# First norm's sums, first loads, context products and VectorE's own operands moved in a two-layer gated transformer kernel

## The chip, the cores and the metric

The kernel runs on one core of a Trainium2 chip, as one program of five instruction streams: TensorE (PE), VectorE (DVE), ScalarE (ACT), GpSimd (POOL) and SyncE (SP), which here only issues transfers. The metric is device time in microseconds, the median of three runs. The profile is of one execution, with a time of its own.

## The reference

x is 128 × 64 tokens of 128 features; four sublayers are added to it, each scaled by tanh of a gate.

```python
x = x + tanh(g_xattn[0]) * L0_xattn(layernorm(x), ctx, ctx)     # 16 heads of 8, among the heads of one token
x = x + tanh(g_ffn[0])   * L0_ffn(layernorm(x))                 # 8 experts, relu, two per token by a hash
x = x + tanh(g_xattn[1]) * L1_xattn(layernorm(x), ctx)          # 64 tokens against 64 of context
x = x + tanh(g_ffn[1])   * L1_ffn(layernorm(x))                 # 8 gated experts + 2 shared, top 2
# L0_xattn, per token l:  q = x Wq, k = ctx Wk, v = ctx Wv, as 16 heads of 8
attn = softmax(einsum('nlhd,nled->nlhe', q, k) / sqrt(8)); out = einsum('nlhe,nled->nlhd', attn, v) @ Wo.T + bo
# L1_xattn:  vk, vv from x;  lk, lv from ctx
a = softmax(vk @ lk.T * 128**-0.5);  out = a @ lv + a @ (a.T @ vv)
```

The first attention compares the 16 heads of one token with one another, so it is no matrix product: each token has 16 × 16 × 8 products for the scores and as many for the values.

## The kernel before

The 8192 tokens are 16 chunks of 512, each four tiles of 128 tokens. The program is unrolled by steps called halves (a tick is two). Every engine walks the same halves, and in each its own short list of calls, so the written order is the order of its instructions; semaphores join the engines.

**Attention.** Half 16(s+1)+k does step k of chunk s. Beside it stands the preparation of chunk p = s+1 (norm, queries, keys and values) and the tail of chunk r = s−1 (output product, residual, second norm, choice of experts). Of the four tiles GpSimd makes three with products of 128x2048: scores by `times_k` (L574), values by `times_v` (L586), through two buffers named prod, so that each product waits until the last but one is reduced. VectorE reduces them (L873 scores, L898 values) and makes the fourth tile itself (`own_times_k` L854, `own_times_v` L862). For that tile keys and values stand in PSUM: `own_keys_values` (L846) copies them there. VectorE also does the statistics of all norms: for the first norm at k = 2, L817 to L827, through PSUM (named YD). GpSimd raises the variance to the power −1/2 (L562) and scatters rows by expert (L596). The four blocks are of chunks up to 3, 7, 11, 15; at each end VectorE computes a table.

**Experts of the first layer** run in twelve steps per block, placed in halves 108 to 356, on TensorE (L1276, L1290) with relus on ScalarE (L683).

**Second layer.** Chunk c's cross attention (C) starts at half 272 + 16c; its context products are lk (L1391) and lv (L1415, beside L1416 in one bank). The gated experts (D) start at half 288 + 16d: up and gate products (L1244 to L1246), silu on ScalarE (L705), hidden product on VectorE (L1095), output (L1328), and for every unit the weighted sum on VectorE (L1110). While C and D of neighbouring chunks overlap, TensorE goes from one to the other by this order alone.

**Start.** SyncE issues eight loads (L453 to L460) and four stores of zeros (L463); TensorE waits for all weights and constants first.

Names: x0 the chunk's rows, q_sb queries and later values' sums, s scores, kv_sb keys and values, MA and MC the banks of the attention's products, xrow the rows of the residual, nmean, ve and rstd a norm's mean (negative), variance and its root's inverse, x3 and xd the D stage's input and sum.

## Time and profile before

| | |
|---|---|
| median of three runs | 1307.96 us (1305.18 to 1308.02) |
| profiled execution | 1305.32 us, its span 1303.6 us |
| granted TensorE clock, mean | 0.959 |
| PE busy | 1113.0 us (85%) |
| DVE busy | 1010.9 us (78%) |
| ACT busy | 586.5 us (45%) |
| POOL busy | 637.0 us (49%) |

The shares are means over stages with different limits, so they are to be read by stretch: attention alone up to about 223 us, attention beside experts to 623 us, then the second layer. "Idle before, releaser" in a row is the time for which the engine had nothing to do, and what ended it.

### The profile page before, as it was taken

Reading aid. Unit: us, or ns where it says so; the run is one execution under the profiler, and the core shown is the slowest. Engines: PE = TensorE matmul, PEld = TensorE weight load, DVE = VectorE, ACT = ScalarE, POOL = GpSimd, SP = SyncE. Lnnn points to the kernel's source line nnn. Section 1 sums busy time; section 2 is a strip of 40 time slices with the busy share of each in tenths; the row PEclk is TensorE's granted clock in tenths of the full one; section 3 lists DMA queues with packets and bytes.
Section 4 is the critical chain, followed back from the end, with each engine's and each line's share of the span. In section 5 each row is a group of like instructions: output and inputs, shape, how many; then the busy total and the mean of one; then the engine's idle time right before and its main releaser. Section 6 shows DMA issues by size and latency. Waiting matters only on the chain.

```text
span 1303.6 us, 23736 instructions
## 1 busy us (share of the span) xinstructions
PE 1113.0 (85%) x7464; PEld 960.2 (74%) x7464; DVE 1010.9 (78%) x2393; ACT 586.5 (45%) x1506; POOL 637.0 (49%) x377
## 2 busy tenths in 40 slices
PE   5145544899969998799889999999999999999998
PEld 3133333789858988688788888889888888888887
DVE  2999999989999899898537444445688888888887
ACT  2212222465636555355454645454344444444443
POOL 4889997898788987899340110101011111111200
PEclk9999985799989999799899999999999999999999
DMA  6101112889748886589666255552000000000000
GB/s 226 49 25 41 40 41 73 264 269 284 224 151 263 278 253 208 187 240 294 189 198 206 78 176 160 174 162 79 22 25 25 25 25 25 26 25 25 26 9 17
DMA packets 125035, 166.41 MB, mean 128 GB/s; under 512 B 10032, under 2 KB 67568, under 8 KB 124912
## 3 DMA queue, kind: packets, MB, share of 16 engines
q1 hardware_dynamic: 119792, 152.31, 38.1%
q0 software_dynamic: 5120, 12.59, 2.9%
q8 instruction: 61, 1.00, 0.3%
q14 instruction: 62, 0.51, 0.1%
HBM read 137.60 MB, written 27.26 MB: 126 GB/s over the span
## 4 chain that ended last, share of the span: by engine, by line
PE 56%; DVE 25%; issue 8%; POOL 7%; ACT 2%; DMA 1%; SPq 0%; DVEq 0%; POOLq 0%; ACTq 0%
PE ZB L1276 8%; DVE q_sb L898 6%; PE YB L1290 6%; PE YD L1328 5%; DVE s L873 4%; PE ZD L1244 4%; PE ZD L1246 4%; PE ZD L1245 4%; POOL prod L586 3%; PE YB L1328 3%; PE ZB L1244 2%; DVE own_prod L862 2%; PE ZB L1246 2%; PE ZB L1245 2%; POOL xs L596 2%
## 5 line engine op out<-in xcount | busy, mean ns | idle before, releaser
L562 POOL TENSOR_TENSOR rstd<-ve,neghalf 128x4 f32<-128x4 f32 x64 | 65.6, 1025 | 516.6 <-DVE ve L827 515.2
L683 ACT ACTIVATE hid<-ZB,w2b 128x128 f32<-128x128 f32 x768 | 215.8, 378 | 159.0 <-PE YB L1290 78.5
L574 POOL TENSOR_TENSOR prod<-q_sb,kv_sb 128x2048 f32<-128x2048 f32 x48 | 216.3, 4507 | 51.9 <-DVE q_sb L898 31.6
L586 POOL TENSOR_TENSOR prod<-s,kv_sb 128x2048 f32<-128x2048 f32 x48 | 215.2, 4505 | 10.6 <-DVE q_sb L898 10.5
L1276 PE MATMUL ZB<-bt,w1b 128*128 128x128 f32 x1536 | 213.2, 284 | 4.9 <-ACT hid L683 4.7
L1276 PEld LDWEIGHTS ZB<-bt,w1b 128*128 128x128 f32 x1536 | 197.0, 200 | 8.5 <-issue 8.0
L1290 PE MATMUL YB<-w2b,hid 128*128 128x128 f32 x1024 | 141.4, 282 | 0.0
L1290 PEld LDWEIGHTS YB<-w2b,hid 128*128 128x128 f32 x1024 | 129.1, 194 | 14.2 <-ACT hid L683 8.0
L705 ACT ACTIVATE own_prod<-ZD 128x512 f32<-128x512 f32 x102 | 61.1, 599 | 154.6 <-PE ZD L1246 152.3
L1095 DVE TENSOR_TENSOR prod<-own_prod,ZD 128x512 f32<-128x512 f32 x102 | 69.5, 682 | 75.0 <-ACT own_prod L705 51.7
L1110 DVE SCALAR_TENSOR_TENSOR own_prod<-YD,gate,own_prod 128x128 f32<-128x128 f32 x320 | 89.7, 342 | 46.5 <-PE YD L1328 44.6
L873 DVE TENSOR_REDUCE s<-prod 128x256 f32<-128x2048 f32 x48 | 108.2, 2275 | 5.4 <-POOL prod L574 5.4
L898 DVE TENSOR_REDUCE q_sb<-prod 128x128 f32<-128x2048 f32 x48 | 109.1, 2273 | 1.4 <-POOL prod L586 1.0
L1244 PE MATMUL ZD<-ut_hi,w_hi 128*128 128x512 f32 x204 | 89.0, 436 | 0.0
L1328 PEld LDWEIGHTS YD<-w2u_sb,prod 128*128 128x128 f32 x640 | 79.8, 192 | 9.9 <-issue 4.7
L1328 PE MATMUL YD<-w2u_sb,prod 128*128 128x128 f32 x640 | 85.0, 276 | 2.4 <-DVE own_prod L1110 1.5
L1246 PE MATMUL ZD<-ut_lo,w_hi 128*128 128x512 f32 x204 | 80.5, 394 | 0.0
L1245 PE MATMUL ZD<-ut_hi,w_lo 128*128 128x512 f32 x204 | 80.4, 394 | 0.0
L596 POOL DMA_INDIRECT xs<-xrow,slots x64 | 63.3, 989 | 23.1 <-issue 17.7
L608 POOL DMA_INDIRECT x<-x2d,homes x64 | 61.8, 966 | 23.6 <-issue 23.3
L1290 PE MATMUL ZD<-w2b,hid 128*128 128x128 f32 x512 | 69.3, 279 | 0.0
L1290 PEld LDWEIGHTS ZD<-w2b,hid 128*128 128x128 f32 x512 | 62.6, 192 | 5.8 <-issue 3.0
(249 smaller groups left out, 2321.0 us busy)
## 6 DMA issues: line engine op xcount, KB each, us to landing
w2b<-in_w SPq DMA_DIRECT2D x96, 516.0 KB
w1b<-in_w SPq DMA_DIRECT2D x96, 512.0 KB
xb<-xs SPq DMA_DIRECT2D x96, 128.0 KB
ctx_t<-in_ctx SPq DMA_DIRECT2D x32, 256.0 KB
x2d<-x2s SPq DMA_DIRECT2D x48, 128.0 KB
x<-in_x SPq DMA_DIRECT2D x16, 256.0 KB
xs<-zrow SPq DMA_DIRECT2D x4, 1024.0 KB, 10.5
xrow<-in_x SPq DMA_DIRECT2D x16, 256.0 KB, 3.6
```

The lines of the kernel that those rows point to most:

```text
L574: pool.tensor_tensor(out=prod[:, t % 2, :].rearrange("p (h e d) -> p h e d", h=HEADS, e=HEADS), in0=q.unsqueeze(2).broadcast_to([P, HEADS, ...
L586: pool.tensor_tensor(out=prod[:, (t + 1) % 2, :].rearrange("p (h d e) -> p h d e", h=HEADS, e=HEADS), in0=s0[:, t, :, :].unsqueeze(2).broa ...
L683: act.activation(hid[n % 2][:, j, k * RT:(k + 1) * RT], ZB[j // 2][:, at:at + RT], ACT.Relu, bias=w2b[t % 3][:, k, e, FJ * D + j:FJ * D + ...
L873: dve.tensor_reduce(out=s0[:, t, :, :].rearrange("p h e -> p (h e)"), in_=src.rearrange("p (g d) -> p g d", d=HD), axis=X, op=ALU.add).the ...
L898: dve.tensor_reduce(out=o_sb[a % 2][:, t, :], in_=src.rearrange("p (g e) -> p g e", e=HEADS), axis=X, op=ALU.add).then_inc(av_sum.sem, 1)
L1110: last = dve.scalar_tensor_tensor(out=xd[:, j, :], in0=b[:, j * P:(j + 1) * P], scalar=gate[:, j, u - SHARED:u - SHARED + 1], in1=xd[:, j, ...
L1244: pe.matmul(dst, l_hi, r_hi, start=True, stop=False)
L1245: pe.matmul(dst, l_lo, r_hi, start=False, stop=False)
L1246: return pe.matmul(dst, l_hi, r_lo, start=False, stop=True)
L1276: last = pe.matmul(ZB[j // 2][:, at:at + RT], w1b[t % 2][:, k, e, j * P:(j + 1) * P], bt[t % 2][:, k * RT:(k + 1) * RT], start=True, stop= ...
L1290: last = pe.matmul(b[:, k * D:(k + 1) * D], hid[n % 2][:, f, k * RT:(k + 1) * RT], w2b[t % 3][:, k, e, f * D:(f + 1) * D], start=False, st ...
L1328: last = pe.matmul(b[:, js], hu[(d * UNITS + u) % 3][:, js], w2u_sb[:, u, :], start=True, stop=True)
```

## The change

1. The order of the first loads: rows, biases, context and 384 columns of the weights first, the rest behind them. The zero stores go to halves 24 to 36, the constants of VectorE to half 16, and TensorE's wait for the other weights to half 24. The first chunk has an order of its own.
2. For chunks from 1 on ScalarE makes the first norm's sums: `sums_of_rows` at k = 12 of the step before, `sums_of_squares` at k = 0. VectorE turns them into mean and variance with two operations of 128x4.
3. VectorE's own keys and values are read from kv_sb, which ScalarE now fills for all four tiles; `own_keys_values` goes. The choice of experts needs two operations less.
4. The context products of all 16 chunks are made in halves 31 to 91 (`languages`), stored to DRAM (lk_d, lv_d) and loaded in C.
5. In D from chunk 5 on, ScalarE weighs units 2 to 5 (`unit_weighed`), GpSimd adds them (`add_unit`), and VectorE's other sums come one half later.

```diff
+LANG_AT = [16 * (c // 4) + 31 + (0, 2, 9, 12)[c % 4] for c in range(NC)]
+LANG = {half: c for c, half in enumerate(LANG_AT)}
...
+BY_ACT = (2, 3, 4, 5)
+WEIGHED = {(d, u): (d - FIRST_ACT) * len(BY_ACT) + i + 1 for d in range(FIRST_ACT, NC) for i, u in enumerate(BY_ACT)}
+STEP = {}
+for _d in range(NC):
+    for _u in range(1, UNITS):
+        if (_d, _u) not in WEIGHED:
+            STEP[_d, _u] = len(STEP) + 1
...
+            sp.dma_start(x0[:], x_v[0]).then_inc(ld_x.sem, 16)
+            sp.dma_start(bias_raw[:], bias_rows[0:BG].unsqueeze(0)).then_inc(s_bias, 16)
+            sp.dma_start(ctx_t[:], ctx_in[:, 0:CH]).then_inc(ld_ca.sem, 16)
+            sp.dma_start(ws[:, 0:WO], w_small[:, 0:WO]).then_inc(s_ws, 16)
...
-            sp.dma_start(x0[:], x_v[0]).then_inc(ld_x.sem, 16)
-            sp.dma_start(ctx_t[:], ctx_in[:, 0:CH]).then_inc(ld_ca.sem, 16)
-            sp.dma_start(ws[:], w_small).then_inc(s_ws, 16)
+            sp.wait_ge(s_ws, 16)
+            sp.dma_start(ws[:, WO:WSMALL], w_small[:, WO:WSMALL]).then_inc(s_ws, 16)
...
-            for b in range(len(BLOCKS)):
-                sp.dma_start(xs[b][8 * GT * RT:ROWS].rearrange("(k p) d -> p k d", p=P),
-                             zrow[:].unsqueeze(1).broadcast_to([P, SPARE, 2 * D])).then_inc(st_zero.sem, 16)
...
                 if k == 9 and has(p + 1):
                     filled(sp, "xt0", p)
                     sp.dma_start(x0[:], x_v[p + 1]).then_inc(ld_x.sem, 16)
+                if 24 <= half < 24 + 4 * len(BLOCKS) and half % 4 == 0:
+                    sp.dma_start(xs[half // 4 - 6][8 * GT * RT:ROWS].rearrange("(k p) d -> p k d", p=P),
+                                 zrow[:].unsqueeze(1).broadcast_to([P, SPARE, 2 * D])).then_inc(st_zero.sem, 16)
...
+                for c in range(NC):
+                    if half == (LANG_AT[c - 2] + 1 if has(c - 2) else LANG_AT[c] - 4):
+                        if has(c - 2):
+                            sp.wait_ge(pe_lang.sem, pe_lang.at(c - 2))
+                        sp.dma_start(ctx_l[c % 2], ctx_in[:, c * CH:(c + 1) * CH]).then_inc(ld_cl[c % 2].sem, 16)
...
+                    sp.dma_start(lk_d[c], lang_k[c % 2]).then_inc(st_lang[c % 2].sem, 16)
+                    sp.dma_start(lv_d[c], lang_v[c % 2]).then_inc(st_lang[c % 2].sem, 16)
...
-                                filled(sp, "val", c - 1)
-                            sp.dma_start(ctx2_t[:], ctx_in[:, c * CH:(c + 1) * CH]).then_inc(ld_cc.sem, 16)
+                                filled(sp, "sc", c - 1)
...
+                            sp.dma_start(lk_t[:], lk_d[c]).then_inc(ld_lk.sem, 16)
+                            if has(c - 1):
+                                emptied(sp, "val", c - 1)
+                            sp.dma_start(lv_sb[:], lv_d[c]).then_inc(ld_lv.sem, 16)
...
+            def add_unit(d, u):
+                n = WEIGHED[d, u]
+                if u == BY_ACT[0]:
+                    pool.wait_ge(xd_s.sem, STEP[d, 1])
+                else:
+                    pool.wait_ge(added.sem, n - 1)
+                pool.wait_ge(y_s.sem, n)
+                pool.tensor_tensor(out=xd[:], in0=xd[:], in1=y_act[n % 2][:], op=ALU.add).then_inc(added.sem, 1)
...
+            def sums_of_rows(c):
+                if has(c - 1):
+                    act.wait_ge(ln_stats[0].sem, ln_stats[0].at(c - 1))
+                act.wait_ge(ld_x.sem, ld_x.at(c))
+                for j in range(TILES):
+                    last = act.activation(spill[:, j, :], x0[:, j, :], ACT.Copy, accum_out=sums0[:, 0, j:j + 1])
+                last.then_inc(sums0_s.sem, 1)
+            def sums_of_squares(c):
+                act.wait_ge(ln_stats[0].sem, ln_stats[0].at(c, 1))
+                for j in range(TILES):
+                    last = act.activation(spill[:, j, :], x0[:, j, :], ACT.Square, bias=nmean[:, 0, j:j + 1], accum_out=sums0[:, 1, j:j + 1])
+                last.then_inc(sums0_s.sem, 1)
...
+                if half and has(p - 2):
+                    act.wait_ge(own_av.sem, own_av.at(p - 2))
+                act.activation(kv_sb[p % 2][:, 2 * half:2 * half + 2, :].rearrange("p j d -> p (j d)"), b[:],
+                               ACT.Copy).then_inc(free_of(f"kv{half}", p), 1)
...
+                act.wait_ge(pe_f.sem, pe_f.at(d, u))
+                b = unit_sums[SUM[d, u][0]]
+                for j in range(TILES):
+                    last = act.activation(y_act[n % 2][:, j, :], b[:, j * P:(j + 1) * P], ACT.Copy, scale=gate[:, j, u - SHARED:u - SHARED + 1])
+                last.then_inc(y_s.sem, 1)
...
                     plain(ot[:], "ot", r)
+                if half == 4:
+                    normed(0, lambda j: xn0[:, j, :], lambda j: x0[:, j, :], 0)
...
+                if half == 14:
+                    weights()
...
+                if k == 12 and has(p + 1):
+                    sums_of_rows(p + 1)
+                if k == 0 and has(p) and p > 0:
+                    sums_of_squares(p)
...
+            def later_consts():
...
+            def means_of_rows(c):
+                dve.wait_ge(sums0_s.sem, sums0_s.at(c - 1, 1))
+                dve.wait_ge(ln_rstd[0].sem, ln_rstd[0].at(c - 1))
+                dve.tensor_scalar(nmean[:, 0, :], sums0[:, 0, :], -1.0 / D, None, ALU.mult).then_inc(ln_stats[0].sem, 1)
+            def variances_of_rows(c):
+                dve.wait_ge(sums0_s.sem, sums0_s.at(c - 1))
+                dve.tensor_scalar(ve[:, 0, :], sums0[:, 1, :], 1.0 / D, EPS, ALU.mult, ALU.add).then_inc(ln_stats[0].sem, 2)
...
-            def own_keys_values(p):
-                kv_part_of = filled(dve, "kv1", p)
-                dve.wait_ge(kv_part.sem, kv_part.at(p))
-                if has(p - 1):
-                    dve.wait_ge(own_av.sem, own_av.at(p - 1))
-                dve.tensor_copy(kv_own, kv_part_of[:, (PT - 2) * 2 * D:2 * 2 * D]).then_inc(free_of("kv1", p), 1)
...
-                kk = kv_own[:, 0:D].rearrange("p (e d) -> p e d", e=HEADS)
+                kk = kv_sb[a % 2][:, PT, 0:D].rearrange("p (e d) -> p e d", e=HEADS)
...
-                v = kv_own[:, D:2 * D].rearrange("p (d e) -> p d e", e=HEADS)
+                v = kv_sb[a % 2][:, PT, D:2 * D].rearrange("p (d e) -> p d e", e=HEADS)
...
-                hs = sm("hsum").unsqueeze(2).broadcast_to([P, TILES, TRUNC_MAX])
-                th_ = thr[:].unsqueeze(1).broadcast_to([P, TILES, TRUNC_MAX])
-                dve.tensor_tensor(out=hge[:], in0=hs, in1=th_, op=ALU.is_ge).then_inc(s, 1)
-                dve.scalar_tensor_tensor(out=hle, in0=hs, scalar=-1.0, in1=th_, op0=ALU.mult, op1=ALU.is_ge).then_inc(s, 1)
+                hs = sm("hsum").unsqueeze(2).broadcast_to([P, TILES, 2 * TRUNC_MAX])
+                th_ = thr[:].unsqueeze(1).broadcast_to([P, TILES, 2 * TRUNC_MAX])
+                dve.tensor_tensor(out=hge[:], in0=hs, in1=th_, op=ALU.is_gt).then_inc(s, 1)
+                dve.wait_ge(pick.sem, pick.at(r, 2))
+                dve.tensor_reduce(out=sm("htr"), in_=hge[:], axis=X, op=ALU.add).then_inc(s, 1)
...
+                dve.wait_ge(ld_lv.sem, ld_lv.at(c))
+                dve.tensor_tensor(out=u_sb[:], in0=tiles(b), in1=tiles(lv_sb), op=ALU.add).then_inc(free_of("val", c), 1)
...
+                back = 1 if d >= FIRST_ACT else 0
+                if UNIT_OUT.get(pos) == 1:
+                    unit_sum(d, 1)
+                elif (d, UNIT_OUT.get(pos - back)) in STEP and UNIT_OUT[pos - back] > 1:
+                    unit_sum(d, UNIT_OUT[pos - back])
...
+                if half == 16:
+                    later_consts()
...
-                    if has(p):
-                        dve.wait_ge(ld_x.sem, ld_x.at(p))
-                        norm_stats(0, lambda j: x0[:, j, :], p)
+                    if has(p) and p > 0:
+                        variances_of_rows(p)
...
+                if k == 14 and has(p + 1):
+                    means_of_rows(p + 1)
...
-                    if has(p):
-                        own_keys_values(p)
...
-                    pe.wait_ge(xd_s.sem, earlier + 1)
+                    if earlier in WEIGHED:
+                        pe.wait_ge(y_s.sem, WEIGHED[earlier])
+                    else:
+                        pe.wait_ge(xd_s.sem, STEP[earlier])
...
+            def languages(c):
...
+                pe.wait_ge(ld_cl[c % 2].sem, ld_cl[c % 2].at(c // 2))
+                pe.matmul(ZB[0][:], ws[:, WLK:WLK + P], ctx_l[c % 2], start=True, stop=True).then_inc(pe_lang.sem, 1)
+                bias_rows_of(ZB[1][:, :], BLV, D, TILES)
+                by_token(ZB[1], ctx_l[c % 2], WLV, D, start=False).then_inc(pe_lang.sem, 1)
...
-                        pe.matmul(b[:, js], ctx2_t[:, js], ws[:, WLV:WLV + D], start=True, stop=False)
-                        last = pe.matmul(b[:, js], blockdiag[:, j, :], vv_sb[:, j, :], start=False, stop=True)
+                        last = pe.matmul(b[:, js], blockdiag[:, j, :], vv_sb[:, j, :], start=True, stop=True)
...
-            pe.wait_ge(s_rows, 16)
-            pe.wait_ge(s_dve0, DVE_CONSTS)
-            pe.wait_ge(s_w2u, 16)
+            pe.wait_ge(s_dve0, 1)
...
+                if half == 24:
+                    pe.wait_ge(s_ws, 32)
+                    pe.wait_ge(s_dve0, DVE_CONSTS)
+                    pe.wait_ge(s_w2u, 16)
+                if half in LANG:
+                    languages(LANG[half])
```

VectorE in an attention cycle, behind its own value product, to the reciprocal and the copy. Before:

```order
L862 TENSOR_TENSOR own_prod<-s,YD 128x2048 [waits exp0]
L906 TENSOR_TENSOR q_sb<-q_sb,YD 128x256 [waits rec0_s,av_sum]
L888 TENSOR_REDUCE sum<-s 128x32 [waits exp0]
L890 RECIPROCAL YD<-sum 128x32 [waits rec0_s]
L846 COPY YD<-MC 128x256 [waits own_av,kv_part,mc_full]
```

and now:

```order
L978 TENSOR_TENSOR own_prod<-s,kv_sb 128x2048 [waits exp0]
L946 TENSOR_SCALAR nmean<-sums 128x4 [waits ln_rstd0,sums0_ready]
L1022 TENSOR_TENSOR q_sb<-q_sb,YD 128x256 [waits rec0_s,av_sum]
L1004 TENSOR_REDUCE sum<-s 128x32 [waits exp0]
L1006 RECIPROCAL YD<-sum 128x32 [waits rec0_s]
```

The mean of the next chunk stands directly behind the value product, and the copy is gone.

VectorE a few instructions on, from the reduction of its own value product to the first reductions of scores (YD is in PSUM, stats and sums in SBUF). Before:

```order
L898 TENSOR_REDUCE q_sb<-own_prod 128x128 [waits own_av]
L906 TENSOR_TENSOR q_sb<-q_sb,YD 128x256 [waits rec0_s,av_sum]
L817 BN_STATS stats<-x 128x6 [waits ld_x]
L817 BN_STATS stats<-x 128x6 x3
L821 BN_AGGR YD<-stats 128x2 [waits ln_stats0]
L821 BN_AGGR YD<-stats 128x2 x3
L826 TENSOR_SCALAR nmean<-YD 128x4 [waits ln_rstd0,ln_stats0]
L827 TENSOR_SCALAR ve<-YD 128x4
L873 TENSOR_REDUCE s<-prod 128x256 [waits pool_qk] x2
```

and now:

```order
L1014 TENSOR_REDUCE q_sb<-prod 128x128 [waits pool_av]
L1014 TENSOR_REDUCE q_sb<-own_prod 128x128 [waits own_av]
L1022 TENSOR_TENSOR q_sb<-q_sb,YD 128x256 [waits rec0_s,av_sum]
L950 TENSOR_SCALAR ve<-sums 128x4 [waits sums0_ready]
L989 TENSOR_REDUCE s<-prod 128x256 [waits pool_qk] x2
```

Seven instructions' worth of statistics became one operation, with both sides in SBUF.

TensorE in the last stage, where the next chunk's cross attention begins (prod and xn are norm outputs, transposed here; L1391 is lk). Before:

```order
L1235 MATMUL MC<-ident,prod 128x128 [waits ln_done3,mc_free]
L1235 MATMUL MC<-ident,prod 128x128 x3
L1391 MATMUL MA<-ctx_t,ws 128x512 [waits ld_ctx_c,ma_free]
L1328 MATMUL YB<-w2u_sb,prod 128x128 [waits hu_ready,xd_step]
L1328 MATMUL YB<-w2u_sb,prod 128x128 x3
L1235 MATMUL MC<-ident,xn 128x128 [waits ln_done2,mc_free]
L1235 MATMUL MC<-ident,xn 128x128 x3
```

and now:

```order
L1362 MATMUL MA<-ident,prod 128x128 [waits ln_done3,ma_free]
L1362 MATMUL MA<-ident,prod 128x128 x3
L1460 MATMUL YB<-w2u_sb,prod 128x128 [waits hu_ready,xd_step]
L1460 MATMUL YB<-w2u_sb,prod 128x128 x3
L1362 MATMUL MC<-ident,xn 128x128 [waits ln_done2,mc_free]
L1362 MATMUL MC<-ident,xn 128x128 x3
L1460 MATMUL YD<-w2u_sb,prod 128x128 [waits hu_ready,xd_step]
```

The product lk is gone between the two transposes; some of the L1460 products now wait for y_by_act instead of xd_step.

## Rows read from the trace of the kernel before

**Rows 1.** Busy time by stretch: stretch, us; PE, PEld, DVE, ACT, POOL, PEclk, DMA, GB/s

```profile
38.00:183.00 145.00, 66.98 (x200) 45.92 (x200) 139.61 (x209) 31.73 (x66) 129.08 (x54) 1.00 0.13 39
...
700.00:913.00 213.00, 209.12 (x1554) 187.62 (x1554) 104.77 (x330) 106.42 (x297) 25.26 (x32) 1.00 0.49 150
948.00:1272.00 324.00, 314.87 (x2126) 271.89 (x2125) 263.88 (x866) 153.36 (x271) 58.20 (x75) 1.00 0.09 24
```

**Rows 2.** Timeline of POOL: start us, us, engine, line, operation, idle before

```profile
38.31 4.51 POOL L586 TENSOR_TENSOR prod<-s,kv_sb 128x2048 f32<-128x2048 f32 x1
...
147.94 13.36 POOL L586 TENSOR_TENSOR prod<-s,kv_sb 128x2048 f32<-128x2048 f32 x3
161.26 9.04 POOL L574 TENSOR_TENSOR prod<-q_sb,kv_sb 128x2048 f32<-128x2048 f32 x2
...
172.12 4.51 POOL L574 TENSOR_TENSOR prod<-q_sb,kv_sb 128x2048 f32<-128x2048 f32 x1 [0.57 <-DVE s L873]
...
182.96 4.49 POOL L586 TENSOR_TENSOR prod<-s,kv_sb 128x2048 f32<-128x2048 f32 x1
...
223.21 13.36 POOL L586 TENSOR_TENSOR prod<-s,kv_sb 128x2048 f32<-128x2048 f32 x3
...
377.63 13.41 POOL L586 TENSOR_TENSOR prod<-s,kv_sb 128x2048 f32<-128x2048 f32 x3
...
532.18 8.96 POOL L586 TENSOR_TENSOR prod<-s,kv_sb 128x2048 f32<-128x2048 f32 x2
...
570.82 4.52 POOL L586 TENSOR_TENSOR prod<-s,kv_sb 128x2048 f32<-128x2048 f32 x1
```

**Rows 3.** Timeline of DVE over the same cycle

```profile
159.09 2.28 DVE L862 TENSOR_TENSOR own_prod<-s,YD 128x2048 f32<-128x2048 f32 x1
161.29 0.41 DVE L906 TENSOR_TENSOR q_sb<-q_sb,YD 128x256 f32<-128x256 f32 x1
...
162.60 0.37 DVE L846 COPY YD<-MC 128x256 f32<-128x256 f32 x1
162.88 0.18 DVE L950 TENSOR_TENSOR spick<-MA,oh_all 128x32 f32<-128x32 f32 x1
...
163.40 2.27 DVE L898 TENSOR_REDUCE q_sb<-prod 128x128 f32<-128x2048 f32 x1
...
168.24 0.86 DVE L817 BATCH_NORM_STATS2 stats<-x 128x6 f32<-128x128 f32 x4
...
169.70 4.47 DVE L873 TENSOR_REDUCE s<-prod 128x256 f32<-128x2048 f32 x2
```

**Rows 4.** Line L922: its durations (min/median/max), and one of them on DVE's timeline

```profile
L922 DVE COPY oh_all<-base x4: 155/257/2229, 84.4 to 542.3; 128x8 f32<-128x8 f32 x4
...
229.93 2.23 DVE L922 COPY oh_all<-base 128x8 f32<-128x8 f32 x1
```

**Rows 5.** Timelines of SP, PE and POOL at the start

```profile
4.85 9.30 SPq L463 DMA_DIRECT2D xs<-zrow  x4
...
11.03 0.76 PE L1341 MATMUL MC<-bias_hi,ones_r 1*128 1x512 f32 x1 [11.03 <-DMA w2u_sb<-in_w2u]
...
23.73 4.49 POOL L574 TENSOR_TENSOR prod<-q_sb,kv_sb 128x2048 f32<-128x2048 f32 x1 [10.14 <-ACT q_sb L661]
```

**Rows 6.** Timelines of PE and ACT in the last stage

```profile
1000.86 0.38 PE L1415 MATMUL MC<-ws,ctx_t 128*128 128x128 f32 x2
1001.07 0.39 PE L1416 MATMUL MC<-vv_sb,blockdiag 128*128 128x128 f32 x2
...
1013.12 1.02 PE L1391 MATMUL MA<-ctx_t,ws 128*128 128x512 f32 x2
...
1015.59 0.63 PE L1235 MATMUL MC<-ident,xn 128*128 128x128 f32 x4 [0.56 <-ACT xn L655]
...
1013.81 1.63 ACT L655 ACTIVATE xn<-x,nmr,rstd 128x128 f32<-128x128 f32 x4
```

**Rows 7.** Timeline of SP beside the experts

```profile
342.76 0.44 SPq L475 DMA_DIRECT2D x<-in_x  x1
```

More of the change, by code:

```diff
@@ L469, in _ @@
                 p, a, r = s + 1, s, s - 1
[L470 removed]
+                if k == (7 if p > 0 else 10) and has(p + 1):
                     filled(sp, "kv1", p)
@@ L637, in _ @@
                             gather(c, (2, 3))
+                for d, kd in d_parts(tick):
+                    u = UNIT_OUT.get(2 * kd + later - 1)
+                    if (d, u) in WEIGHED:
+                        add_unit(d, u)
         @block.scalar
```

158 lines of the change are left out of this document (99 added, 59 removed).

## The prediction

> **What bounds the kernel now.** I read the table of stretches first [rows 1], then the timelines of GpSimd (POOL) and VectorE (DVE) over one attention cycle [rows 2, 3], one odd instruction of VectorE [rows 4], the start [rows 5], and TensorE (PE) in the last stage [rows 6]. The table splits the program in two. In 38 to 183 us VectorE is busy 139.6 of 145 us and GpSimd 129.1, TensorE only 67: attention is a two-engine loop. From 700 us on TensorE decides alone: 209.1 of 213 us, and 314.9 of 324 in the last stage [rows 1].
>
> The loop's period is the distance between two first value products of GpSimd, 147.94 to 182.96: 35.02 us, and nothing but this loop runs there. Each product takes 4.45 us. Three of values run back to back from 147.94, two of keys follow at 161.26, the third of keys starts only at 172.12, after 0.57 us of waiting for VectorE's reduction L873 [rows 2]. VectorE in turn waits only some tenths per cycle for a product. So both engines are within 0.6 us of being the bound, and whatever delays either one in this loop is paid in full.
>
> **The change, part by part.**
>
> 1. *VectorE's work per chunk shrinks.* Gone are the norm statistics of the first norm (168.24 to 169.70, 1.46 us), the copy L846 (162.60 to 162.88, 0.28 us) [rows 3] and two of the small operations of the expert choice, about 0.27 us in all. Two operations of 128x4 are added, means_of_rows behind own_times_v and variances_of_rows behind head_scale. By start-to-start time they cost 0.08 us each, an estimate from their size. Taken alone this is 1.85 us less on VectorE, of which GpSimd's own loop (35.02 less its 0.57 wait) lets through about 0.6 us a chunk.
>
> 2. *But the two new operations have another form.* The old ones read PSUM; the new ones read SBUF and write SBUF. The trace has one operation of that kind inside attention, the copy L922, four times, each 128x8: 155 ns at the least, 257 in the middle, 2229 at the most [rows 4]. The long one started at 229.93 on VectorE. GpSimd had started three value products at 223.21, each 4.45 us, so its second ended at 223.21 + 8.9 = 232.1, and the copy ended at 229.93 + 2.23 = 232.16. It read as a wait until GpSimd's product was over. I take it that a one-source operation from SBUF to SBUF waits for the running product, and apply this to both new operations.
>
> Where do they fall? Before, own_times_v started at 159.09 and the next operation at 161.29; GpSimd's first key product started at 161.26 [rows 2, 3]. The new means_of_rows takes the place at 161.29, 0.03 us too late: it waits for the key product, to 161.26 + 4.5 = 165.7, which is 4.4 us. The tail behind it (161.29 to 163.40, less the copy 0.28: 1.83 us) then ends at 167.5, and the third reduction of values at 167.5 + 2.2 = 169.7. GpSimd's second key product waits for that reduction since it reuses its buffer: it starts at 169.8, not at 165.7. Reduction of the own product and scale bring VectorE to 172.3; there variances_of_rows finds that second product running, until 174.2. The first reduction of key products ends at 174.3 + 2.2 = 176.5, and with it the third key product starts at about 176.6, not at 172.12. That is 4.5 us late, and the cycle grows from 35.02 to about 39.6, **+4.6 us**.
>
> The waits act where a chunk two ahead exists, so in 14 of 15 intervals between first value products. By groups:
> - The first three intervals, 38.31 to 147.94 [rows 2]: 109.6 us, 4.6 over three bare cycles of 35.02. Half of that excess I take as covered by the new waits: 3 × 4.6 − 2.3 = +11.5.
> - One bare interval (147.94 to 182.96): +4.6. One with the block's table (182.96 to 223.21, 40.25 us): +4.4.
> - Two blocks of four intervals beside the experts, 223.21 to 377.63 and on to 532.18: 154.4 us each, 14.3 over four bare cycles. The table's 5.2 of it stays; of the other 9.1, which are waits for other engines, 2.4 stays as an estimate: 4 × 39.6 + 7.6 = 166.0, so +11.6 each, +23.2.
> - The last one (532.18 to 570.82, 38.6 us) to 40.3: +1.7.
>
> Sum for attention: 11.5 + 4.6 + 4.4 + 23.2 + 1.7 = **+45.4 us**.
>
> 3. *VectorE's own products now take both operands from SBUF.* No row shows such an operation beside a product of GpSimd; before, one operand was always in PSUM. Bounds: nothing, as the same operation runs at 2.2 us now, or a wait like that of L922, which is rival A below. I take nothing, since the rows show the wait only for a one-source form.
>
> The Trainium skill ("SBUF — State Buffer", section "Who interferes with whom") says more: a VectorE instruction with two SBUF inputs, or a one-source one that can use both ports, shares an exclusive port pair with GpSimd, and whoever comes second is blocked entirely. The second half agrees with the 2229 ns of L922; the first half speaks against this change and no row here shows it. With it the result would be rival A's.
>
> 4. *ScalarE (ACT) makes the sums.* Eight passes of 128x128 per chunk, 1.63 us for four [rows 6]: 3.3 us on an engine that is under half busy, hidden in the free stretches. Beside the experts it can hurt: the load of x is issued at 342.76 in the place where ScalarE makes relus without a break [rows 7], and sums_of_rows stands ahead of relus in its queue. An x that lands some 3 to 4 us later holds them, and with them TensorE. Bounds 0 to 8 us over all chunks. In the main case VectorE is late by more than that, so I take 0; in rival C it counts 8.
>
> 5. *Start.* TensorE starts at 11.03, after the last of the eight first loads; the first key product at 23.73; SyncE's queue is held 9.3 us by four stores of zeros [rows 5]. With 384 columns of the weights awaited instead of everything, TensorE can start about 5 us earlier, and the queries are made before the second half of keys and values, which takes 2 us more out of the chain: **−7 us** (5 to 9). The weights deferred are needed at half 24, behind the first products. The four stores of zeros move to halves 24 to 36; the first that waits for them is SyncE's padding at the end of the first block, so nothing is late by it. On SyncE's queue they now stand among loads of context and x that are issued early, which I cost at nothing, with 1 us as the bound.
>
> 6. *Context products.* lk (two passes, 1013.12 to 1013.98, 0.86 us) and lv (four passes of 0.22, as 1000.86 to 1001.07 [rows 6], 0.9 us) leave each of 16 late chunks and go where TensorE is half idle; 28 us are hidden there, with ScalarE's copies. In the five chunks before the last stage, where TensorE is 98% busy, they save 5 × 1.76 = 8.8; I take 7.5, since some of these chunks overlap waits. In the last stage lk saves nothing: behind it TensorE waits 0.56 us for ScalarE's xn at 1015.59 [rows 6], and would wait 1.4 instead. lv saves 0.9 less what the new hand-over costs.
>
> 7. *Units weighed by ScalarE and added by GpSimd.* This takes four operations from VectorE for each of four units. VectorE is not the bound there (263.9 of 324 us [rows 1]). TensorE now waits for ScalarE's 1.63 us instead of VectorE's similar step, with one half less of room, and I charge 0.3 us a chunk: 11 × (0.9 − 0.3) = −6.6. Bounds −12 to +5. Parts 6 and 7 together: **−14 us**.
>
> Sum against the profiled run's own 1305.3 us: 45.4 − 7 − 14.1 = +24.3, so 1329.6. The median of the runs lies 2.7 over the profiled one, so the forecast is **1332 us**.
>
> **Rivals.**
>
> *A, both forms wait.* own_times_v at 159.09 waits for the third value product until 161.26 and keeps GpSimd out to 163.5; GpSimd's key product runs 163.5 to 168.0, and means_of_rows behind it to 168.0. That is 2.3 us more than in the main case; own_times_k, beside GpSimd's power of the variance before the next value product, adds 0.7: cycle 42.6, +3.0 on the main case. 3 × 3.0 + 2 × 3.0 + 8 × 3.0 + 3.0 = 42 on top: **1374 us**. For it: copy L846 pays 0.28 us a chunk [rows 3] for nothing but an operand in PSUM. Against: no row shows such a wait.
>
> *B, the tie is won.* means_of_rows gets in ahead of the key product at 161.26; the two starts lie 0.03 us apart. Then it waits for nothing, variances_of_rows waits 2.3 us, most of it behind GpSimd's own loop; the cycle is 35.4: about +5 in attention, **1292 us**. From a lead of 0.03 us it decides for each cycle.
>
> *C, no waits* (the other side: faster). The 2.23 us of L922 had another cause. Attention gives 14 × 0.6 = 8 us, which ScalarE's late x takes back (part 4); start −7, parts 6 and 7 −14: 1305.3 − 21 + 2.7 = **1287 us**. For it: VectorE's saved 1.85 us a chunk is real. Against: the end of L922 fits GpSimd's to 0.1 us.
>
> **How the numbers follow.** Main case 0.30 (own range 1318 to 1348: each wait may be 1 us shorter, the D stage may give nothing), A 0.28, B 0.12, C 0.30. Predicted is the main case, 1332. The range takes in A and C: C less 6 for ScalarE's stalls not coming, 1281; A plus 14 for the last stage giving nothing, 1388. A change of 0.3%, 4 us, is about what can be told from none. Slower is main and A, 0.57 with a 0.01 from them near zero; faster is B and C less 0.04 where their savings fail, 0.38; within 0.3% 0.05.
>
> **What would show it.** The two operations of 128x4 at means_of_rows and variances_of_rows: near 0.15 us each in B's and C's case, medians of 4.4 and 1.9 us in mine. own_times_v: 2.2 us, or 4.4 in A. Distance between first value products in the bare stretch: 39.6, 42.6 (A), 35.4 (B), 34.4 (C). First key product at about 17 us. Last stage: about 0.6 us less a chunk. The forecast is wrong if the first of these is short.

## The result

The changed kernel takes 1404.96 us, median of four runs (1401.13 to 1409.36), against 1306.92 us before (1305.18 to 1308.02): a ratio of 1.0753, with a 95% interval of 1.0717 to 1.0788. It is 98 us slower. The sign was forecast; the size was not: 1332 us was predicted, and 1405 lies above the range's end of 1388.

The profiled execution took 1404.14 us with a span of 1401.8 us. The first view is the source view of lines of the changed kernel: durations in ns, least, median and most, then the first and last start. L946 is the new mean, L950 the new variance, L978 VectorE's own product of values, L970 that of keys, L621 GpSimd's key products, L633 its value products.

```profile
L946 DVE TENSOR_SCALAR nmean<-sums x15: 1668/4437/4466, 16.5 to 651.4; 128x4 f32<-128x4 f32 x15
L950 DVE TENSOR_SCALAR ve<-sums x15: 170/2084/2109, 23.2 to 662.4; 128x4 f32<-128x4 f32 x15
L978 DVE TENSOR_TENSOR own_prod<-s,kv_sb x16: 2281/2850/4384, 47.8 to 737.8; 128x2048 f32<-128x2048 f32 x16
L970 DVE TENSOR_TENSOR own_prod<-q_sb,kv_sb x16: 2279/2282/5914, 34.3 to 713.5; 128x2048 f32<-128x2048 f32 x16
L621 POOL TENSOR_TENSOR prod<-q_sb,kv_sb x48: 4471/4516/6569, 13.6 to 703.7; 128x2048 f32<-128x2048 f32 x48
L633 POOL TENSOR_TENSOR prod<-s,kv_sb x48: 4471/4507/6604, 30.4 to 729.8; 128x2048 f32<-128x2048 f32 x48
```

An operation on 512 numbers takes 4.4 us, and that is the wait which the forecast named. But the two products of VectorE are stretched too, up to 4.4 and 5.9 us, and GpSimd's up to 6.6, which the forecast had put at nothing. The bare cycle (147.94 to 182.96 in the kernel before, beside no experts and no table) shows both. Here are VectorE's and then GpSimd's timeline of the changed kernel in the stretch that answers to [rows 2, 3]:

```profile
174.19 2.29 DVE L1014 TENSOR_REDUCE q_sb<-prod 128x128 f32<-128x2048 f32 x1 [0.43 <-POOL prod L633]
176.39 4.35 DVE L978 TENSOR_TENSOR own_prod<-s,kv_sb 128x2048 f32<-128x2048 f32 x1
180.67 4.45 DVE L946 TENSOR_SCALAR nmean<-sums 128x4 f32<-128x4 f32 x1
185.03 0.41 DVE L1022 TENSOR_TENSOR q_sb<-q_sb,YD 128x256 f32<-128x256 f32 x1
...
191.70 2.08 DVE L950 TENSOR_SCALAR ve<-sums 128x4 f32<-128x4 f32 x1
193.69 4.47 DVE L989 TENSOR_REDUCE s<-prod 128x256 f32<-128x2048 f32 x2
...
203.97 2.28 DVE L970 TENSOR_TENSOR own_prod<-q_sb,kv_sb 128x2048 f32<-128x2048 f32 x1
```

```profile
165.20 13.39 POOL L633 TENSOR_TENSOR prod<-s,kv_sb 128x2048 f32<-128x2048 f32 x3
178.56 6.52 POOL L621 TENSOR_TENSOR prod<-q_sb,kv_sb 128x2048 f32<-128x2048 f32 x1
189.28 4.47 POOL L621 TENSOR_TENSOR prod<-q_sb,kv_sb 128x2048 f32<-128x2048 f32 x1 [4.19 <-DVE q_sb L1014]
...
196.13 4.51 POOL L621 TENSOR_TENSOR prod<-q_sb,kv_sb 128x2048 f32<-128x2048 f32 x1 [0.99 <-DVE s L989]
...
203.46 0.96 POOL L643 DMA_INDIRECT xs<-xrow,slots  x1 [0.30 <-issue]
204.73 2.36 POOL L643 DMA_INDIRECT xs<-xrow,slots  x1 [0.30 <-issue]
207.12 1.04 POOL L608 TENSOR_TENSOR rstd<-ve,neghalf 128x4 f32<-128x4 f32 x1
208.24 0.20 POOL L610 TENSOR_TENSOR nmr<-nmean,rstd 128x4 f32<-128x4 f32 x1
208.39 8.94 POOL L633 TENSOR_TENSOR prod<-s,kv_sb 128x2048 f32<-128x2048 f32 x2
```

Read them side by side. VectorE's product is ready at 176.39, but GpSimd's third value product runs until 178.6: VectorE comes to its next operation at 180.67, 4.3 us later instead of 2.2. GpSimd's key product, ready at 178.56, takes 6.52 us: 2.1 us of waiting for VectorE and 4.4 of work. The mean, ready at 180.67, then waits until this key product is over (185.08), the variance waits from 191.70 to the end of the next (193.75). Three times in a cycle VectorE waits for GpSimd, and twice GpSimd for VectorE: at the key product, and at the last scatter, which takes 2.36 us instead of 0.96 while VectorE makes its product of keys (203.97). The cycle, from 165.20 to 208.39, is 43.2 us; it was 35.02 [rows 2].

By the distances between first value products (L633 here, L586 in rows 2) the whole program divides as follows, in us:

| part | before | changed | difference | forecast |
|---|---|---|---|---|
| up to the first value product | 38.3 | 30.4 | −7.9 | −7 |
| first three intervals | 109.6 | 134.8 | +25.2 | +11.5 |
| bare interval | 35.0 | 43.2 | +8.2 | +4.6 |
| interval with table | 40.2 | 48.4 | +8.1 | +4.4 |
| two blocks of four beside experts | 154.4, 154.6 | 186.3, 192.9 | +70.2 | +23.2 |
| last two intervals | 38.6, 34.2 | 42.9, 37.0 | +7.1 | +1.7 |
| from the last first value product to the end | 698.6 | 686.0 | −12.6 | −14 |

The two parts outside attention came as forecast. All of the miss is in attention, +118.7 us instead of +45.4.

The blocks also show something that the bare cycle doesn't. These rows are of the waits of ScalarE and TensorE in the changed kernel, 250 to 720 us (total, times, longest). L729 is the sum of squares, L756 the relus, L1405 the experts' first product.

```profile
ACT x L729 <- DVE nmean L946: 61.8, 7, 14.5
```

```profile
PE ZB L1405 <- ACT hid L756: 39.7, 17, 5.8
```

ScalarE stood 61.8 us at the sum of squares, waiting for the mean that VectorE brought late, with relus queued behind it; TensorE stood 39.7 us for relus (3.1 us in the kernel before, 223 to 623 us).

And TensorE itself was slower there. These are the two blocks of the kernel before and then of the changed kernel, with the columns of [rows 1]:

```profile
223.21:377.63 154.42, 140.15 (x1013) 124.61 (x1011) 143.40 (x246) 82.65 (x264) 133.19 (x57) 0.93 0.76 234
377.63:532.18 154.55, 141.17 (x1011) 125.11 (x1012) 142.00 (x247) 82.19 (x264) 133.31 (x57) 0.93 0.76 235
```

```profile
256.76:443.03 186.27, 151.47 (x1018) 133.56 (x1018) 170.52 (x203) 94.31 (x328) 148.55 (x57) 0.86 0.62 195
443.03:635.92 192.89, 157.34 (x1015) 138.76 (x1016) 172.63 (x203) 94.63 (x328) 148.97 (x58) 0.82 0.60 189
```

In the kernel before TensorE is busy nine tenths of a block. For nearly the same number of matmuls it is busy 11 and 16 us longer in the changed kernel, at a granted clock of 0.86 and 0.82 instead of 0.93.

### The profile page after: what moved, and what is told of

It is laid out like the page before. It is cut to its first block, busy times and chain, and to the rows that moved or that the text cites. A ratio compares the mean times of both kernels' runs of the same rounds, so it can differ in the third digit from the quotient of the medians.

```text
span 1401.8 us, 24127 instructions
## 1 busy us (share of the span) xinstructions
PE 1180.8 (84%) x7496; PEld 997.6 (71%) x7496; DVE 1083.4 (77%) x2050; ACT 686.3 (49%) x1938; POOL 751.8 (54%) x422
## 3 DMA queue, kind: packets, MB, share of 16 engines
q1 hardware_dynamic: 129154, 169.10, 38.3%
## 4 chain that ended last, share of the span: by engine, by line
PE 52%; DVE 28%; POOL 7%; issue 6%; ACT 3%; SPq 1%; DMA 1%; DVEq 0%; POOLq 0%; another core or an unknown queue 0%; ACTq 0%
PE ZB L1405 8%; PE YB L1419 6%; DVE q_sb L1014 5%; PE YD L1460 5%; DVE nmean L946 4%; DVE s L989 4%; POOL prod L633 4%; DVE own_prod L978 3%; PE ZD L1371 3%; PE ZD L1372 3%; PE ZD L1373 3%; PE YB L1460 3%; DVE own_prod L970 3%; POOL xs L643 2%; PE ZB L1371 2%
## 5 line engine op out<-in xcount | busy, mean ns | idle before, releaser
L621 POOL TENSOR_TENSOR prod<-q_sb,kv_sb 128x2048 f32<-128x2048 f32 x48 | 246.5, 5137 | 96.1 <-DVE q_sb L1014 74.5
L756 ACT ACTIVATE hid<-ZB,w2b 128x128 f32<-128x128 f32 x768 | 216.3, 377 | 139.4 <-PE YB L1419 59.1
L1405 PE MATMUL ZB<-bt,w1b 128*128 128x128 f32 x1536 | 226.2, 296 | 43.4 <-ACT hid L756 43.3
L1405 PEld LDWEIGHTS ZB<-bt,w1b 128*128 128x128 f32 x1536 | 208.5, 211 | 47.7 <-issue 47.3
L633 POOL TENSOR_TENSOR prod<-s,kv_sb 128x2048 f32<-128x2048 f32 x48 | 227.5, 4760 | 17.9 <-DVE q_sb L1014 17.7
L608 POOL TENSOR_TENSOR rstd<-ve,neghalf 128x4 f32<-128x4 f32 x64 | 68.6, 1071 | 267.0 <-DVE ve L941 263.9
L665 POOL TENSOR_TENSOR own_prod<-own_prod,prod 128x512 f32<-128x512 f32 x44 | 56.5, 1285 | 208.6 <-ACT prod L788 208.4
L1014 DVE TENSOR_REDUCE q_sb<-prod 128x128 f32<-128x2048 f32 x48 | 109.0, 2271 | 11.7 <-POOL prod L633 11.6
L1233 DVE SCALAR_TENSOR_TENSOR own_prod<-YD,gate,own_prod 128x128 f32<-128x128 f32 x232 | 65.1, 342 | 40.3 <-PE YD L1460 39.5
L1460 PE MATMUL YD<-w2u_sb,prod 128*128 128x128 f32 x640 | 86.0, 277 | 4.7 <-DVE own_prod L1233 3.8
L1460 PEld LDWEIGHTS YD<-w2u_sb,prod 128*128 128x128 f32 x640 | 79.2, 191 | 9.7 <-DVE own_prod L1233 5.6
L643 POOL DMA_INDIRECT xs<-xrow,slots x64 | 70.7, 1104 | 23.1 <-issue 17.6
L1419 PE MATMUL ZD<-w2b,hid 128*128 128x128 f32 x512 | 76.6, 298 | 0.0
L1419 PEld LDWEIGHTS ZD<-w2b,hid 128*128 128x128 f32 x512 | 69.8, 210 | 6.7 <-issue 3.7
```

The lines of the kernel that those rows point to most:

```text
L621: pool.tensor_tensor(out=prod[:, t % 2, :].rearrange("p (h e d) -> p h e d", h=HEADS, e=HEADS), in0=q.unsqueeze(2).broadcast_to([P, HEADS, ...
L633: pool.tensor_tensor(out=prod[:, (t + 1) % 2, :].rearrange("p (h d e) -> p h d e", h=HEADS, e=HEADS), in0=s0[:, t, :, :].unsqueeze(2).broa ...
L643: pool.indirect_dma_start(xs[b], bass.IndirectOffsetOnAxis(ap=slots[:, r, j:j + 1], axis=0), xrow[r % 2][:, j, :], None).then_inc(st_xs[r ...
L756: act.activation(hid[n % 2][:, j, k * RT:(k + 1) * RT], ZB[j // 2][:, at:at + RT], ACT.Relu, bias=w2b[t % 3][:, k, e, FJ * D + j:FJ * D + ...
L1014: dve.tensor_reduce(out=o_sb[a % 2][:, t, :], in_=src.rearrange("p (g e) -> p g e", e=HEADS), axis=X, op=ALU.add).then_inc(av_sum.sem, 1)
L1405: last = pe.matmul(ZB[j // 2][:, at:at + RT], w1b[t % 2][:, k, e, j * P:(j + 1) * P], bt[t % 2][:, k * RT:(k + 1) * RT], start=True, stop= ...
```

## The experiments

Each kernel was run beside the kernel before. Their statements were written before they ran. The edits are shown against the changed kernel, except where it is said otherwise.

**e1: the own operands in PSUM again, the small operations as changed**

```diff
-                act.activation(kv_sb[p % 2][:, 2 * half:2 * half + 2, :].rearrange("p j d -> p (j d)"), b[:],
-                               ACT.Copy).then_inc(free_of(f"kv{half}", p), 1)
+                n = PT - 2 if half else 2
+                act.activation(kv_sb[p % 2][:, 2 * half:2 * half + n, :].rearrange("p j d -> p (j d)"), b[:, 0:n * 2 * D],
+                               ACT.Copy).then_inc(kv_part.sem if half else free_of(f"kv{half}", p), 1)
...
+                dve.tensor_copy(kv_own, kv_part_of[:, (PT - 2) * 2 * D:2 * 2 * D]).then_inc(free_of("kv1", p), 1)
...
-                kk = kv_sb[a % 2][:, PT, 0:D].rearrange("p (e d) -> p e d", e=HEADS)
+                kk = kv_own[:, 0:D].rearrange("p (e d) -> p e d", e=HEADS)
```

> The changed kernel with VectorE's own keys and values copied to PSUM again (ScalarE copies three tiles, VectorE the fourth), all else as changed. Its products then have one operand in SBUF; the mean and the variance keep both sides in SBUF. Theory 1 (every VectorE operation that reads twice from SBUF, or goes from SBUF to SBUF, shuts out and is shut out by GpSimd's products): only the two small waits are left, own_times_v takes 2.28 us each time, GpSimd's key products 4.5 us at most; bare cycle 39.5 us (43.2 changed, 35.0 before), time about 1405 - 14 x 3.7 = 1353 us. Rival (the small operations alone make all of it, the products' longer times are a mere consequence): the cycle stays at 43, time near 1400.

Measured: 1336.93 us, ratio 1.0243 (1.0226 to 1.026), 16 us less than stated. This is the case that I had forecast for the changed kernel. On VectorE's and GpSimd's timelines:

```profile
165.87 2.28 DVE L985 TENSOR_TENSOR own_prod<-s,YD 128x2048 f32<-128x2048 f32 x1
168.06 4.49 DVE L946 TENSOR_SCALAR nmean<-sums 128x4 f32<-128x4 f32 x1
...
179.41 2.09 DVE L950 TENSOR_SCALAR ve<-sums 128x4 f32<-128x4 f32 x1
```

```profile
154.66 13.42 POOL L634 TENSOR_TENSOR prod<-s,kv_sb 128x2048 f32<-128x2048 f32 x3
168.05 4.47 POOL L622 TENSOR_TENSOR prod<-q_sb,kv_sb 128x2048 f32<-128x2048 f32 x1
176.99 4.48 POOL L622 TENSOR_TENSOR prod<-q_sb,kv_sb 128x2048 f32<-128x2048 f32 x1 [4.47 <-DVE q_sb L1021]
```

The own product takes 2.28 us again and the key product 4.47. The mean is ready at 168.06, GpSimd's key product at 168.05: the tie is lost by 0.01 us, as forecast, and costs 4.4 us. The bare cycle is 40.0 us (forecast 39.6). Over the whole of attention the median wait is shorter, since in the other cycles the mean came up to 1.8 us after the start of the key product; it never came ahead of it:

```profile
L946 DVE TENSOR_SCALAR nmean<-sums x15: 443/3155/4501, 19.3 to 589.7; 128x4 f32<-128x4 f32 x15
```

The rival, that the small operations make all of the loss, falls: 68 us went away with the own operands, where the statement had 52.

**e2: mean and variance with an operand in PSUM, the own operands as changed**

```diff
-                dve.tensor_scalar(nmean[:, 0, :], sums0[:, 0, :], -1.0 / D, None, ALU.mult).then_inc(ln_stats[0].sem, 1)
+                dve.scalar_tensor_tensor(out=nmean[:, 0, :], in0=sums0[:, 0, :], scalar=-1.0 / D, in1=sm("zero"), op0=ALU.mult, op1=ALU.add).then_inc(ln_stats[0].sem, 1)
```

and the variance in the same way with `sm("eps")`; both constants stand in PSUM.

> The changed kernel with mean and variance made by a two-input form whose second input, zero or epsilon, stands in PSUM; VectorE's own products still read SBUF twice. Theory 1: the mean takes 0.2 us instead of 4.4, own_times_v still 2.3 to 4.4 us, GpSimd's first key product up to 6.6; bare cycle 38.1, time about 1405 - 14 x 5.1 = 1334 us. Rival (two-input reads from SBUF cost nothing by themselves): cycle 34.4, own_times_v 2.28 throughout, time about 1283.

Measured: 1328.96 us, ratio 1.0199 (1.0158 to 1.0239); 1334 had been stated. The mean takes 146 ns in the median and at most 158, in the same place of the same queue:

```profile
L950 DVE SCALAR_TENSOR_TENSOR nmean<-sums,YD x15: 143/146/158, 17.4 to 577.7; 128x4 f32<-128x4 f32 x15
L982 DVE TENSOR_TENSOR own_prod<-s,kv_sb x16: 2282/4158/4373, 47.8 to 658.9; 128x2048 f32<-128x2048 f32 x16
```

The own product of values still waits, median 4.2 us. The bare cycle is 37.8 us. So each form waits by itself. The edit changes the kind of operation together with the place of an operand; the kernel before tells them apart. There the first two norms' means were the same TENSOR_SCALAR of 128x4 with its source in PSUM, about half of them begun while a product of GpSimd was running (one at 169.56, beside the product of 161.26 to 170.30), and none took more than 163 ns:

```profile
L826 DVE TENSOR_SCALAR nmean<-YD x32: 160/161/163, 11.9 to 649.7; 128x4 f32<-128x4 f32 x32
```

**e3: both together**

> Both of these together: no operation of VectorE in attention takes two operands from SBUF or goes from SBUF to SBUF, except the table's copy. All other parts of the change stay. Theory 1: bare cycle 34.4, and with the waits of VectorE gone ScalarE's squares don't hold relus for long; time about 1285 us, below the kernel before (1307). Rival (ScalarE's sums in its queue, ahead of relus, cost by themselves in the blocks of experts): bare cycle 34.4, but the blocks stay 5 to 15 us longer than the 154.4 of before, time 1300 to 1315.

Measured: 1291.18 us, ratio 0.9899 (0.9863 to 0.9934), faster than the kernel before. The products and the two small operations are no longer stretched, GpSimd's value products take at most 4.54 us; only the table's copy (L922 before), left as it was, still takes up to 1.80 us.

```profile
L989 DVE TENSOR_TENSOR own_prod<-s,YD x16: 2275/2278/2280, 48.9 to 625.5; 128x2048 f32<-128x2048 f32 x16
```

The two intervals ahead of the table are 35.0 and 36.0 us, not 34.4, and the blocks are 155.4 and 160.0 us. The time is 6 us above the 1285 stated and below the rival's 1300: the waits are gone, and something in the blocks is left.

The four kernels, changed, e1, e2 and e3, differ in two edits alone, so they price what comes of both waits together: 1404.96 − 1336.93 − 1328.96 + 1291.18 = 30 us beyond the sum of each alone. By the distances between first value products 29 of it lie in the two blocks of four.

**e4: as e1, with the first norm's statistics on VectorE again**

```diff
                 if k == 14 and has(p + 1):
-                    means_of_rows(p + 1)
...
-                        variances_of_rows(p)
+                        dve.wait_ge(ld_x.sem, ld_x.at(p))
+                        norm_stats(0, lambda j: x0[:, j, :], p)
```

> As the first kernel of this call (own operands in PSUM), with the first norm's statistics on VectorE again and no sums on ScalarE. What is left of the change: the start, the shorter expert choice, the context products, the units weighed by ScalarE. Theory 1: bare cycle 34.7 to 35.0 as before, blocks as before (154), start and second layer as in the changed kernel, 8 + 12 us less than before: 1287 us. If ScalarE's sums cost in the blocks, this kernel is faster than the third by what they cost; if they only help, it is 0 to 8 us slower.

ScalarE's sums are gone as well. Measured: 1289.72 us, ratio 0.9881 (0.9865 to 0.9898); 1287 had been stated. The same two intervals are 35.8 and 35.1, the blocks 154.3 and 153.9. Without the sums on ScalarE the kernel is as fast as with them: the 1.46 us that they take from VectorE per chunk bring nothing. Where they went is seen in VectorE's largest wait, 38 to 600 us, of the kernel before, of e3 and of e4. It is the residual (xrow) waiting for the attention's output product on TensorE:

```profile
DVE xrow L913 <- PE MA L1240: 10.8, 8, 3.7
```

```profile
DVE xrow L1040 <- PE MA L1380: 40.5, 13, 5.8
```

```profile
DVE xrow L1032 <- PE MA L1371: 17.8, 8, 3.7
```

In e3 VectorE comes to this place earlier and waits 40.5 us in all instead of 10.8 (18.1 with 7.3 us at the same operation for which the view names no engine). I read this as the next limit: the chain of output transpose, copy and product didn't get shorter. No run shortened it, so that is not shown.

**e5: e4 without the units weighed by ScalarE**

```diff
-FIRST_ACT = next(d for d in range(NC) if 2 * C0[d] + 16 > EXPERTS_END + 4)
+FIRST_ACT = NC
```

> As e4_stats_dve, but ScalarE weighs no unit in the last stage; VectorE makes all unit sums again. If the weighing gives nothing (VectorE is not the bound there, my step 7), this is 1286 to 1290 us, as e4 or up to 3 us faster, since TensorE doesn't wait for ScalarE's slower hand-over. Rival (it is what brings the last stage's gain): 1295 or more.

Measured: 1292.53 us, ratio 0.9888 (0.9871 to 0.9904). From the last first value product to the end it takes 690.6 us, e4 685.1, in one execution of each. The medians lie only 2.8 us apart and the intervals of the two ratios overlap, so a gain of 3 to 6 us from the weighing is possible and not shown. What is shown is that it doesn't cost the 3 us with which I had charged it. The time lies between the statement's 1290 and its rival's 1295.

**e6: e4 with lk and lv made in the cross attention, as before**

```diff
-LANG = {half: c for c, half in enumerate(LANG_AT)}
+LANG = {}
...
-C_FIRST = {1: "vk", 2: "vv", 4: "bdt"}
+C_FIRST = {0: "lk", 1: "vk", 2: "vv", 4: "bdt"}
```

> As e4_stats_dve, but the context products lk and lv stay in the cross attention as in the kernel before. If they bring 14 us in the second layer (step 6), the second layer grows by 8 to 14 us and the time is about 1300. In the first chunks the granted clock tells whether these products have to do with its fall to 0.79 (24 to 150 us; 1.00 before): at 1.00 here, they have; attention would then be 1 to 3 us shorter.

Measured: 1302.26 us, ratio 0.9955 (0.9939 to 0.9972). The same last stretch takes 701.5 us, so moving the context products brings 16 us of it beside the weighing (8 to 14 had been stated). The clock answers clearly. These are the rows of the table of stretches, 24 to 150 us, of the kernel before, of e4 and of e6; the number after POOL's is the granted clock:

```profile
24.00:150.00 126.00, 58.01 (x165) 38.79 (x164) 115.25 (x169) 31.14 (x64) 111.92 (x44) 1.00 0.13 38
```

```profile
24.00:150.00 126.00, 94.11 (x304) 57.26 (x304) 119.53 (x178) 44.97 (x87) 108.06 (x44) 0.79 0.46 151
```

```profile
24.00:150.00 126.00, 55.84 (x160) 37.61 (x160) 120.28 (x178) 30.30 (x63) 108.23 (x43) 1.00 0.23 73
```

With the context products there the granted clock of this stretch, a mean between its two levels, is 0.79; without them it is 1.00. But attention from the first to the last first value product takes 566.3 us in e6 and 565.6 in e4, so the lower clock costs nothing that can be seen, where the statement had 1 to 3 us; TensorE is not the limit there.

**e7: the kernel before with the own operands read from SBUF, and nothing else** (the edit is e1's, the other way round)

> The kernel before with this one part of the change: VectorE's own keys and values read from SBUF, ScalarE copying all four tiles, the copy to PSUM gone. Theory 1 (two-input reads from SBUF and GpSimd's products shut each other out): VectorE's product of values 4.35 us instead of 2.28, GpSimd's first key product 6.5, bare cycle 37.8 to 38.5 instead of 35.0, time 1306 + 14 x 3 = 1345 us. Rival (it needs the other parts, as the freed queue slots): no change, 1303.

Measured: 1346.7 us, ratio 1.0314 (1.0265 to 1.0363), as stated. The operand of two products, moved from PSUM to SBUF, costs 39 us, and that although it saves the copy of 0.28 us a chunk. The bare cycle is 38.7 us, just over the 38.5 stated. On GpSimd's timeline there is a second victim; VectorE's own product of keys started at 154.91 (first fence), just ahead of a scatter:

```profile
154.91 2.28 DVE L856 TENSOR_TENSOR own_prod<-q_sb,kv_sb 128x2048 f32<-128x2048 f32 x1
```

```profile
153.97 0.96 POOL L597 DMA_INDIRECT xs<-xrow,slots  x1 [0.30 <-issue]
155.24 2.79 POOL L597 DMA_INDIRECT xs<-xrow,slots  x1 [0.30 <-issue]
158.05 1.05 POOL L562 TENSOR_TENSOR rstd<-ve,neghalf 128x4 f32<-128x4 f32 x1
```

The scatter takes 2.79 us instead of 0.96. In the kernel before, with the operand in PSUM, the same pair ran side by side and the scatter took 0.96:

```profile
180.41 2.28 DVE L854 TENSOR_TENSOR own_prod<-q_sb,YD 128x2048 f32<-128x2048 f32 x1
```

```profile
180.70 0.96 POOL L596 DMA_INDIRECT xs<-xrow,slots  x1 [0.30 <-issue]
```

**e8: e3 with ScalarE's sums for chunks 1 to 6 only**

> As e3_both_psum, but ScalarE makes the first norm's sums only for chunks 1 to 6; from 7 on, where experts run beside attention, VectorE's statistics return. If the sums in ScalarE's queue ahead of relus are what made e3's two expert blocks 155.4 and 160.0 us against 154.3 and 153.9 of e4, these go to 154 to 155 and the time is 1284 to 1288, the fastest of all; if they stay over 157, it was something else.

Measured: 1288.78 us, ratio 0.9856 (0.984 to 0.9872); blocks 155.4 and 156.5 us, both over the 154 to 155 stated. The second block went from 160.0 to 156.5, against 153.9 in e4; the first stayed. So the sums account for 3.5 of the second block's 6.1 us at most, and for nothing in the first; the rest is not explained. It is the lowest ratio of all, but its interval overlaps e4's.

**e9: the changed kernel with the sums of squares one half later**

```diff
-                if k == 0 and has(p) and p > 0:
+                if k == 1 and has(p) and p > 0:
                     sums_of_squares(p)
```

> The changed kernel with ScalarE's sums of squares one half later (k = 1 instead of 0), behind the relus of one more expert step; nothing else moved. In the changed kernel ScalarE waited 61.8 us for the mean there, and TensorE 39.7 us for relus, in 250 to 720 us. If that wait at the head of ScalarE's queue is what the blocks of experts lose beyond the waits between VectorE and GpSimd (186.3 and 192.9 us against 166.7 and 168.0 with the small waits alone), both blocks get 5 to 15 us shorter each, and the time is 1375 to 1395; the bare cycle stays 43.2. If ScalarE's wait is hidden, all stays at 1405.

Measured: 1392.33 us, ratio 1.0669 (1.0648 to 1.069), 12.6 us less than the changed kernel. Blocks 180.2 and 184.8 us, 6 and 8 less. Over 250 to 720 us ScalarE's wait for the mean fell from 61.8 to 15.9 us, TensorE's for relus from 39.7 to 31.6. So ScalarE's wait at the head of its queue does cost, 12.6 us net of what the move itself costs. TensorE's busy time in the blocks fell too, by 5.2 and 4.3 us, at a granted clock of 0.91 and 0.85 instead of 0.86 and 0.82; whether that is a part of the gain or comes of it, no run tells.

**e10: e3 with the same move**

> As e3_both_psum with the same move of the squares. ScalarE waited 24.7 us for the mean there and TensorE 9.0 us for relus. If this is the rest that ScalarE's sums cost, its two blocks go from 155.4 and 160.0 to 154 to 157 and the time to 1286 to 1289 (1291 for e3); if not, no change within 2 us.

Measured: 1300.76 us, ratio 0.9963 (0.9942 to 0.9985): a miss, nearly 10 us slower than e3. Its blocks are 161.8 and 160.7 us. Where VectorE is not late the move has nothing to mend, and it brings the variance, and with it the norm, later. TensorE's wait for relus didn't fall (12.0 us over 200 to 660 us, 9.0 in e3). Which part of the norm's chain makes the 10 us I haven't followed.

## Why the prediction was wrong

**The bound (right).** Attention was read as a loop of two engines within 0.6 us of each other, where every delay is paid in full. Each bare cycle shows it.

**Part 2, the small operations (right; in the bare cycle to 0.5 us).** Forecast 4.4 us for the mean, 1.9 for the variance, cycle 39.6 us. In e1, where they act alone, they take 4.49 and 2.09 in the bare cycle, which is 40.0; the mean's median over all chunks is 3.16. From the first to the last first value product e1 takes 617.2 us, 50.5 more than before, where +45.4 was forecast. All of it came from one odd row, the copy of 2229 ns in [rows 4], set against the end of a product on another engine.

**Part 3, VectorE's own products (wrong: the step that failed).** They were put at nothing, "since the rows show the wait only for a one-source form". They do wait: e7 prices them at 39 us alone, e2 at 38 us over e3, and beside the small operations they cost 68 us, the changed kernel over e1. Of the miss of 73 us these are 68; e1 itself lies 5 us over the 1332 of the forecast. No row of before showed two SBUF operands beside a product of GpSimd; that is a missing row and no sign of a zero. What should have weighed more stood in the profile: the copy L846 [rows 3] paid 0.28 us a chunk for nothing but an operand in PSUM. The rule of the Trainium skill ("SBUF — State Buffer", section "Who interferes with whom") covers both forms, and here both of its halves agree with the runs: 146 ns against 4437 ns for the mean with and without an operand in PSUM, 2.28 against up to 4.38 us for the own product of values. Rival A was this case, with a cycle of 42.6 us; 43.2 was measured. It should have been the likeliest, though its 1374 us is 31 short as well.

**The blocks of experts (wrong in size, in rival A too).** Alone, the two waits cost the blocks 12.3 and 13.4 us (e1, forecast 11.6 each) and 10.5 and 6.9 us (e7); together they cost 31.9 and 38.3, over the sum of 22.8 and 20.3. In the bare cycle they only add up: +5.0 and +3.7 against +8.2. The forecast took 6.7 us of other waits per block as cover, which was about right for the small waits alone: four cycles at +5.0 would be 20 us. Rival A kept this cover once and charged the second wait in full, four cycles at 7.6 less 6.8 us, 23.6 a block. Measured, no cover is left: four bare cycles at +8.2 would be 32.7, the first block has 31.9 and the second 5.6 us more than that. One part is a mechanism that no rival had: ScalarE's sum of squares waits for VectorE's late mean at the head of a queue of relus. In part 4 I had looked only at its wait for x, which made 2.0 us in the blocks; the wait for the mean made 61.8. e9 gives back 12.6 us by moving it one half. Another thing that no rival had is TensorE's own time, 11 and 16 us more in the two blocks at a lower granted clock. One of these two may come of the other; no run here separates them, and the blocks' excess is not divided further.

**Part 1, VectorE's saved work (wrong, and rival C rested on it).** GpSimd's loop was to let through 0.6 us a chunk, 8 us in rival C; the main case hardly used it. e3, with the 1.46 us of the statistics saved, is no faster than e4 (1291.2 against 1289.7 us). VectorE waited longer for the output product instead, at the residual.

**Part 5, the start (right in the sum, by two errors that cancel).** −7 forecast, −7.9 measured. TensorE starts at 6.30 instead of 11.03 [rows 5], as forecast, but the first key product at 13.64 instead of 23.73, where about 17 was forecast; two of these ten microseconds are lost again before the first value product, which was not. In the rows of the changed kernel:

```profile
6.30 0.76 PE L1473 MATMUL MC<-bias_hi,ones_r 1*128 1x512 f32 x1 [6.30 <-DVE bias_lo L908]
```

```profile
13.64 8.93 POOL L621 TENSOR_TENSOR prod<-q_sb,kv_sb 128x2048 f32<-128x2048 f32 x2 [6.41 <-ACT q_sb L734]
```

**Parts 6 and 7 (right in the sum).** −14.1 forecast, −12.6 measured, −13.5 in e4. The context products bring 16 us beside the weighing (e6); 17.4 of the sum were theirs, 7.5 and 11 × 0.9. The weighing, which was charged with 3.3 us, costs nothing and may bring 3 to 6 (e5). But without the moved context products the weighing seems to cost 3 us (701.5 in e6 against 698.6 before), so the shares depend on each other.
